# Audio tower on one core: masked k blocks by DMA, conv and down as rounded products, weights rounded between the first slots

## What is computed

```python
# tokens: a conv of kernel 2 and stride 2, the mean of the pair added, layer norm
x = einsum('btki,oik->bto', xb, conv_w) + conv_b + xb.mean(axis=2)
h = layernorm(x) * gamma + beta
# attention over the batch of 64, 16 heads of 16
q, k, v = split(layernorm(h) @ qkv.T + qkv_bias)
h = h + softmax(q @ k.T / 4) @ v @ out_proj.T + out_bias
# gated feed-forward, weights and activations rounded to FP4 in blocks of 16
def fp4(x):                      # per block of 16
    scale = maximum(max(abs(x)) / 6, 1e-12)
    return GRID[searchsorted(MID, abs(x / scale))] * sign(x) * scale
z = layernorm(h)
g = silu(fp4(z) @ fp4(w_gate).T) * (fp4(z) @ fp4(w_up).T)
h = h + fp4(g) @ fp4(w_down).T
```

## Time and profile before

| | |
|---|---|
| Median of 3 runs | 4660.76 us (4659.73 to 4663.47) |
| The profiled execution | 4667.47 us, of it a span of 4665.6 us |
| PE busy | 4432.7 us, 95% of the span |
| DVE busy | 3333.5 us, 71% |
| ACT busy | 2640.0 us, 57% |
| POOL busy | 1959.1 us, 42% |

### The profile page before, as it was taken

How to read it: one execution, slowest core, us unless ns; L and a number is a source line. 1 busy time by engine, 2 the same in 40 slices (tenths; PEclk the granted TensorE clock), 3 DMA queues, 4 the chain that set the end, 5 groups by cost and what they waited for, 6 DMA issues and landing times.

```text
span 4665.6 us, 119233 instructions
## 1 busy us (share of the span) xinstructions
PE 4432.7 (95%) x43016; PEld 3952.5 (85%) x43016; DVE 3333.5 (71%) x6915; ACT 2640.0 (57%) x5596; POOL 1959.1 (42%) x2582
## 2 busy tenths in 40 slices
PE   3999999999999985999999999999999999999997
PEld 2888888888888864899999999999999999998986
DVE  4888888888888863566666666666666666666665
ACT  2666666666666643455555555555555555555553
POOL 1455555555555531334334334334334334334333
PEclk9999999999999997999999999999999999999998
DMA  2000000000000001000000000000000000000000
GB/s 84 20 24 20 24 24 24 22 22 24 24 24 21 23 15 39 8 8 8 15 9 8 15 9 8 15 9 8 15 9 8 15 9 8 15 9 8 15 5 11
DMA packets 64945, 79.30 MB, mean 17 GB/s; under 512 B 8758, under 2 KB 51126, under 8 KB 64438
## 3 DMA queue, kind: packets, MB, share of 16 engines
q1 hardware_dynamic: 64566, 74.07, 5.4%
HBM read 49.40 MB, written 24.64 MB: 16 GB/s over the span
## 4 chain that ended last, share of the span: by engine, by line
PE 56%; DVE 2%; issue 1%; ACT 1%; POOL 1%; DMA 0%; ACTq 0%; DVEq 0%; SPq 0%; POOLq 0%
PE bA L938 11%; PE bA L939 9%; PE bA L940 9%; PE bS L1223 4%; PE bO L1245 3%; PE bA L1307 3%; PE bB L938 2%; PE bB L1208 2%; PE bB L1209 2%; PE bB L940 2%; PE bB L939 2%; PE bA L1308 2%; PE bT L1261 2%; PE bO L1254 1%; PE bO L1249 1%
## 5 line engine op out<-in xcount | busy, mean ns | idle before, releaser
L1638 POOL TENSOR_TENSOR sqs_lo<-sq,sqs_hi 128x768 fp32r<-128x768 f32 x256 | 477.9, 1867 | 676.7 <-ACT sqs_hi L1358 673.1
L1449 DVE TENSOR_TENSOR qk_lo<-bA,qk_hi 128x384 fp32r<-128x384 f32 x512 | 284.5, 556 | 538.6 <-ACT qk_hi L1358 538.5
L1377 ACT ACTIVATE phi<-bB 128x768 f32<-128x768 f32 x256 | 207.4, 810 | 665.1 <-PE bB L1209 665.1
L1596 POOL TENSOR_TENSOR yT_lo<-tanh_y,yT_hi 128x384 fp32r<-128x384 f32 x256 | 259.4, 1014 | 556.8 <-ACT yT_hi L1358 556.8
L1358 ACT ACTIVATE qk_hi<-bA 128x384 fp32r<-128x384 f32 x512 | 251.6, 491 | 203.7 <-PE bA L940 203.5
L1459 DVE TENSOR_TENSOR aT<-bS,mask 128x1024 f32<-128x1024 f32 x256 | 311.0, 1215 | 2.0 <-PE bS L1228 1.3
L1367 ACT ACTIVATE sq<-bA 128x384 f32<-128x384 f32 x512 | 250.3, 489 | 62.0 <-DVE qk_lo L1449 61.8
L518 PE MATMUL bank<-down_sb,hqT 128*128 128x256 f32 x1128 | 278.7, 389 | 1.0 <-ACT hqT L600 1.0
L616 ACT ACTIVATE kblk<-gu,kb_masked,rowmask 128x128 f32<-128x128 f32 x752 | 271.3, 463 | 8.1 <-PE gu L542 8.1
L518 PEld LDWEIGHTS bank<-down_sb,hqT 128*128 128x128 f32 x1128 | 204.3, 190 | 52.8 <-issue 32.6
L938 PE MATMUL bA<-fc_lo,yT_hi 128*128 128x256 f32 x768 | 230.6, 300 | 12.9 <-ACT pre L1407 6.2
(11 more groups left out here) (245 smaller groups left out, 15104.2 us busy)
## 6 DMA issues: line engine op xcount, KB each, us to landing
xT<-in_x SPq DMA_DIRECT2D x94, 256.0 KB, 2.6
h_scratch<-h SPq DMA_DIRECT2D x188, 64.0 KB, 1.9
hx<-h_scratch SPq DMA_DIRECT2D x32, 256.0 KB, 2.7
out<-res SPq DMA_DIRECT2D x32, 256.0 KB, 2.2
hx<-h_scratch SPq DMA_DIRECT2D x64, 64.0 KB, 2.5
out<-res SPq DMA_DIRECT2D x64, 60.0 KB, 1.8
q<-in_fc_q SPq DMA_DIRECT2D x2, 1024.0 KB, 6.4
wq_sb<-in_wq SPq DMA_DIRECT2D x1, 1024.0 KB, 5.0
```

The lines of the kernel that those rows point to most:

```text
L1449: dve.tensor_tensor(dst, src, hi.bitcast(fp32), ALU.subtract).then_inc(S[done], 1)
L1638: pool.tensor_tensor(sqs[1][:], sq[:], sqs[0][:].bitcast(fp32), ALU.subtract).then_inc(S["sq_lo"], 1)
```

## The change

1. **k by DMA.** qk_product computes k first, into a bank of its own. ACT copies it once into `kT` (two instructions), right after probs_copy. SP then issues eight DMAs, each of 16 partitions, that put kT's pieces into a `kblk` cleared once at the start. scores waits for all eight, besides q.
2. **Conv and down rounded.** Both go over `product3`. x is split by a copy on ACT (`x_copy`) and a subtraction on POOL (`x_low`), a slot ahead; hq's transpose by ACT's copy and a new subtraction on DVE (`hq_low`), between glu_up and h1_add.
3. **Order.** DVE: the maximum of xq, then h2_add, then xq's scales. POOL: hq's scaling ahead of h0b.
4. **Weights between slots.** The prologue's block goes. `slots` calls `weights(t)` ahead of each of the first six slots, and the loads, the rounding (two steps now in place of four, the scalings on POOL, the magnitude on ACT), transposes and splits of the weights are spread over them. SP loads layer 1's 4 MB ahead of slot 5.

The core of the diff:

```diff
+                def k_blocks(t):                                    # SP
+                    wait_step(sp, "qk_copied", t, QK, KC)
+                    for j in range(4):
+                        for r in range(2):
+                            p = slice(64 * r + D0 * j, 64 * r + D0 * (j + 1))
+                            sp.dma_start(kblk[p, :, j, :], kT[p, :, :]).then_inc(S["kblk_ready"], 16)
                 def slot(t, par):
                     if exists(t, -1):
                         load(t + 1, 1 - par)
                     if exists(t, 4):
                         store(t - 4, par)
+                    if exists(t, 0):
+                        k_blocks(t)
+                def weights(t):
...
+                    if t == 5:
+                        for dst, v in (("wq_sb", wq), ("wk_sb", wk), ("wv_sb", wv), ("wo_sb", wo)):
+                            sp.dma_start(w1[dst][:], v.rearrange("(c p) n -> p c n", p=128)).then_inc(w1_loaded, 16)
                 def conv(t, par):                                   # PE
-                    pe.wait_ge(S[f"x_loaded{par}"], t * 8 + (16 - 8 * par))
+                    wait(pe, "x_low", t + 1)
                     for c in range(2 * KC):
-                        last = pe.matmul(cv[:, 0:DM], xT[par][:, c, :], conv_sb[:, c, :], start=c == 0,
-                                         stop=c == 2 * KC - 1)
+                        last = product3(pe, cv[:, 0:DM], [x[:, c, :] for x in xTs], [w[:, c, :] for w in conv_w0],
+                                        c == 0, c == 2 * KC - 1)
                 def scores(t):
                     wait(pe, "qk_copied", t, QK)
+                    wait(pe, "kblk_ready", t, 16 * KB)
                     wait(pe, "att_step", t - 1, ATT)
                 def down(t):
-                    wait(pe, "hqT_copied", t - 3, 2)
+                    wait(pe, "hqT_split", t - 3, 2)
                     for f, (o, w) in enumerate(F0C):
-                        last = pe.matmul(cv[:, 0:DM], hqT[0:w, f, :], down_sb[0:w, f, :], start=f == 0,
-                                         stop=f == len(F0C) - 1)
+                        last = product3(pe, cv[:, 0:DM], [x[0:w, f, :] for x in hqT], [x[0:w, f, :] for x in down_w0],
+                                        f == 0, f == len(F0C) - 1)
                 def qk_product(t):
-                    for w, o in ((q_sb, 0), (k_sb, 256)):
+                    for b, w in ((1, k_sb), (0, q_sb)):
...
-                    last.then_inc(S["qk_done"], 1)
+                        last.then_inc(S["qk_done"], 1)
                 def k_copy(t):                                      # ACT
-                    wait(act, "qk_done", t + 1)
+                    wait_step(act, "qk_done", t, 2, 1)
                     wait(act, "scores_done", t)
                     for c in range(KC):
-                        src = gu[:, 0, 256 + 128 * c:256 + 128 * (c + 1)].rearrange("p (n k) -> p n k", n=2)
-                        for j in range(4):
-                            act.activation(kblk[:, c, :, j, :], src, ACT.Identity, bias=kb_masked[:, c, j:j + 1],
-                                           scale=rowmask[:, j:j + 1]).then_inc(S["qk_copied"], 1)
+                        act.activation(kT[:, c, :], gu[:, 1, 128 * c:128 * (c + 1)], ACT.Identity,
+                                       bias=kb_col[:, c:c + 1]).then_inc(S["qk_copied"], 1)
+                def x_copy(t, par):
+                    act.wait_ge(S[f"x_loaded{par}"], t * 8 + (16 - 8 * par))
+                    wait(act, "conv_done", t)
+                    copy(xTs[0][:], xT[par][:], "x_high")
                 def slot(t, par):                                   # ACT
                     if exists(t, 1):
                         v_copy(t, 1 - par)
+                    if exists(t, -1):
+                        x_copy(t + 1, 1 - par)
...
                         probs_copy(t)
+                    if exists(t, 0):
+                        k_copy(t)
                     if exists(t, 2):
                         xq_magnitude(t)
+                def hq_low(t):                                      # DVE
+                    wait(dve, "hqT_copied", t - 3, 2)
+                    dve.tensor_tensor(hqT[1][:, 0:5, :],
+                                      pt[:].rearrange("p a b -> p (a b)")[:, 0:640].rearrange("p (f t) -> p f t", t=128),
+                                      hqT[0][:, 0:5, :].bitcast(fp32), ALU.subtract).then_inc(S["hqT_split"], 1)
+                    dve.tensor_tensor(hqT[1][0:64, 5, :], pt[0:64, 1, 128:256], hqT[0][0:64, 5, :].bitcast(fp32),
+                                      ALU.subtract).then_inc(S["hqT_split"], 1)
                     if exists(t, 2):                                # DVE's slot
-                        x_st = xq_scales(t - 2)
-                        xq_scaled(x_st)
+                        x_st = xq_amax(t - 2)
                     if exists(t, 4):
                         h2_add(t - 4, par)
+                    if exists(t, 2):
+                        xq_scales(x_st)
+                        xq_scaled(x_st)
+                def x_low(t, par):                                  # POOL
+                    wait(pool, "x_high", t + 1)
+                    pool.tensor_tensor(xTs[1][:], xT[par][:], xTs[0][:].bitcast(fp32), ALU.subtract)\
+                        .then_inc(S["x_low"], 1)
+                def weights(t):                                     # POOL
...
+                    if t == 1:
+                        weight_scaled("gate")
+                        weight_scaled("up")
+                        pool.wait_ge(wfold, 5 + KC)
+                    if t == 2:
+                        weight_values("gate")
+                        weight_values("up")
+                        weight_scaled("down")
+                    if t == 3:
+                        weight_values("down")
```

More of the change, by code:

```diff
@@ L107, in fp4_scales @@
     st.add(dve.reciprocal(inv, inv))
+def fp4_scales(dve, st, x, small, rows, width, gain=1.0):
+    fp4_amax(dve, st, x, small, rows, width)
+    fp4_inverse(dve, st, small, rows, width, gain)
 def fp4_scaled(eng, out, x, small, k, rows, width):
@@ new lines, in layer0 @@
+        wconv, wsmall, wqkv, wout = sem("wconv"), sem("wsmall"), sem("wqkv"), sem("wout")
+        wconst, vones, wfold, vbias = sem("wconst"), sem("vones"), sem("wfold"), sem("vbias")
+        wconv_hi, wconv_lo = sem("wconv_hi"), sem("wconv_lo")
+        wpad, wtrans, whigh, wlow = sem("wpad"), sem("wtrans"), sem("whigh"), sem("wlow")
+        W = {n: {k: sem(f"{n}_{k}") for k in ("loaded", "scales", "scaled", "abs", "round", "ready")}
+             for n in ("gate", "up", "down")}
+        wraw = {"gate": sb("graw", [128, GROUPS, DM]), "up": sb("uraw", [128, GROUPS, DM]), "down": sb("draw", [128, KC, F0])}
@@ L388, in wait_stored, with slots @@
                 eng.wait_ge(S[f"{name}{par}"], t * 16 + (32 - 16 * par))
-        def slots(eng, slot):
+        def slots(eng, slot, weights):
             first = 6
@@ L394, in slots @@
             for t in range(first):
+                weights(t)
                 slot(t, t % 2)
@@ L590, in slot, with weight_rows @@
                         pv_product(t, 1 - par)
-                pe.wait_ge(wfold, 6 + 2 * KC)
-                pe.wait_ge(wcopied, len(JOBS))
-                pe.wait_ge(wlow, 2)
-                slots(pe, slot)
+                def weight_rows(n, c, bank):
+                    o = bank[:].rearrange("p a b -> p (a b)")
+                    for j in range(GROUPS):
+                        rows = 128 if j < GROUPS - 1 else LAST
+                        last = pe.transpose(o[:, 128 * j:128 * j + rows], wraw[n][0:rows, j, 128 * c:128 * (c + 1)],
+                                            ident[0:rows, 0:rows])
+                    last.then_inc(wtrans, 1)
@@ L597, in _ @@
+                slots(pe, slot, weights)
             @block.scalar
@@ L660, in ln1_copy @@
                     copy(ln1T[:], tp[:, 0:256], "ln1T_copied")
+                    if isinstance(t, int) and t == 0:
+                        weight_magnitude("gate")
                 def probs_copy(t):
@@ L894, in _ @@
+                slots(dve, slot, weights)
             @block.gpsimd
```

377 lines of the change are left out of this document (212 added, 165 removed).

## The result

The changed kernel takes 4966.57 us (median of 4 runs, 4961.49 to 4972.83) against 4661.43 (4 runs, 4659.73 to 4663.47) of the kernel before: ratio 1.0655, 95% interval 1.0637 to 1.0673. It is 305 us slower, and 249 us above the upper end of the forecast's range.

A forecast was written before the change was run, and what follows sets the result against it. TensorE was taken to bound the 17.18 us slot, then k's DMA chain at 17.25: +6 us over about 88 slots, -24 from the prologue, -18 in sum, a median of 4643 us, range 4590 to 4718.

The forecast's parts named there:

- What bounds the kernel: First layer's steady loop: TensorE sets today's 17.18 us slot by a small margin, with DVE waiting only four or five times.
- DVE's count: First layer's loop: if the DMA chain is cheap, DVE sets a 16.8 us slot, total 4604; chance 0.27.
- the one for TensorE: First layer's loop: TensorE's work alone gives a 15.9 us slot, total 4527; chance 0.02.
- Part 1: Conv and down as rounded products on TensorE: conv 1.92 to 1.42, down 2.87 to 2.12, 1.25 us less per slot.
- Part 2: DVE between glu_up and h1_add: hq_low adds 0.82 + 0.29 less overlap, 1.0 us, of which 0.41 fills h1_add's wait.
- Part 3: Reordering on POOL and DVE: hq's first rounding step falls from 1.30 to 0.9 us, 0.4 us gone.
- Part 4: k's blocks by DMA: first issue +12.57, issues 0.44 apart, landing 1.45, so T = 17.25, +6 us over about 88 slots.
- Rival C: TensorE in the loop: the wait drops its clock to 1.2 GHz, T about 19, 4800 or more; chance 0.05.
- A: k's DMA chain: dearer, 0.475 per issue and 1.8 to land, T = 17.85, total 4696; chance 0.33.
- The sum: Whole kernel: +6 from the loop and -24 from the prologue give -18, a median of 4643 us.
- Part 5: Weights between slots: first conv about 10 us, seventh near 150, 30 us for weights, 10 us ACT hole; gain taken 24.
- A with the stores in the way: k's DMA chain: dearer DMA prices with the stores also in the way, T = 18.1, total 4718.

The follow-up runs named there:

- k4_dmas: Changed kernel, but SP issues only four of k's eight DMAs, the other blocks staying zero: 4626.41 us, ratio 0.9926.
- k1_dma: Changed kernel, but only one of k's eight DMAs is issued, seven eighths of the blocks staying zero: 4625.67 us, ratio 0.9919.
- warm_wait: Changed kernel, all eight DMAs, plus ten unused fp32 128x128 matmuls on TensorE just ahead of scores' wait for k: 4832.17 us, ratio 1.0368.
- flat_blocks: Changed kernel with kblk laid out so each transfer writes one 1 KB piece per partition instead of two of 512 B: 4960.58 us, ratio 1.0650.
- k_by_act: Changed kernel with ACT's eight masked copies of k back in their old place instead of the DMAs: 4758.27 us, ratio 1.0217.
- two_queues: Changed kernel with four of k's eight DMAs issued by ACT behind its two copies, four by SP: 4952.97 us, ratio 1.0627.
- pool_mask: Changed kernel with k's blocks made by two POOL multiplications of kT with a 0/1 mask instead of the DMAs: 4711.42 us, ratio 1.0112.
- sp4_pool: Changed kernel with SP transferring two of four k blocks, POOL masking the others, layer 1's weight loads one to a slot: 4656.39 us, ratio 0.9988.
- nudged: sp4_pool plus two tiny unused POOL additions ahead of its 128x768 subtraction in each layer 1 slot's last chunk: 4641.49 us, ratio 0.9969.

## Why the prediction was wrong

- **What bounds the kernel, and DVE's count.** Near. Without the chain the slot is 16.67 to 16.69 (k4_dmas, k1_dma); the count for DVE had said 16.8 and the one for TensorE 15.9. That 16.8 fits is in part luck, since TensorE is as full there, and its own count was too low, by 0.47 from part 1 alone.
- **Part 1.** Right in direction, too large: down takes 708.36 - 705.97 = 2.39 (forecast 2.12; before 2.87), conv 714.37 - 712.75 = 1.62 (forecast 1.42; before 1.92), 0.78 us a slot and not 1.25. The price of 0.118 us holds inside a group, but single steps at its start or end, and where the rows change from 128 to 64, take some 0.2. In the changed kernel this is no gain in time, since the wait for k swallows it; where the chain is off the path the slot is 0.5 shorter than before (k4_dmas).

```profile
705.97 0.28 PE L1051 MATMUL bank<-down_lo,hqT_hi 128*128 128x256 f32 x1
...
708.36 0.44 PE L342 MATMUL bank<-ident,ln 128*128 128x128 f32 x2
...
712.75 0.39 PE L1051 MATMUL bank<-conv_lo,xT_hi 128*128 128x256 f32 x1
...
714.37 1.14 PE L351 MATMUL gu<-v_sb,ln1T 128*64 128x128 f32 x16
```

- **Part 2.** Right: 0.82 + 0.27, and h1_add with no wait.
- **Part 3.** Right: hq's first step takes 0.91 instead of 1.30.
- **Part 4, the step that failed, in three terms.** Place and structure were right: scores wait for eight issues in a row and the last landing. (a) The issue. I took 0.44 from one to the next, from 0.35 to 0.48; measured (5.18 - 0.59)/7 = 0.66. That is 1.5 us, and above the range. No row I had was of a transfer between two tensors in SBUF, but the price was in the trace of the kernel before. I took the duration of layer 1's stores (0.35) and a small gap; the time from one start to the next is some 0.57 even there (0.92 less 0.35). Nearer are the two stores of the same slot, 1.18 us together: they start 0.70 apart. (b) The landing. I took 1.45 and measured 1.9, the upper end: 0.45 us. It is what those two stores take as well. The rows of the kernel before, with the second store by itself:

```profile
707.52 0.48 SPq L414 DMA_DIRECT2D h_scratch<-h  x1
...
2057.51 0.92 SPq L1174 DMA_DIRECT2D out<-res  x2
...
h_scratch<-h SPq DMA_DIRECT2D x188, 64.0 KB, 1.9
```

By 0.70 and 1.9 the chain gives T = 12.57 + 4.90 + 1.9 + 0.15 = 19.52, and the sum 4843; warm_wait, the same chain at full clock, has 18.99 and 4832. The Trainium skill gives 2.0 us whatever the size ("DMA: Bandwidth & Descriptors", section "Anatomy of one DMA"), measured there on transfers that GpSimd issues. The trace shows 1.9 for SP's, and I had weighed size and target above it.

(c) The clock. Rival C had the mechanism and a chance of 0.05, since I judged it by a wait of 0.7 to 1 us, that is, by my own mid value of the chain. The wait is 2.4 us. At the dear end of my range (18.0) it would have been 1.4 to 1.7, and at 19.52 some 3: C was no rival of A, it grows with A. Measured price 1.49 us a slot (warm_wait). In the slot the first issue comes at +13.85, and in warm_wait at +12.40 (710.94 against scores at 717.53 - 18.99), where I had +12.57.

- **The sum again with measured terms:** 13.85 + 4.59 + 1.9 + 0.15 = 20.49; the mean slot is 20.48. With warm_wait's first issue it is 12.40 + 4.59 + 1.9 + 0.15 = 19.04; warm_wait has 18.99.
- **Part 5.** First conv at 8.77 (forecast 10), seventh at 157.84 (150), 17.4 us gained of the forecast 24 to 25. ACT's hole is 14.6 us and not 10: the load of x's tile is itself held 4.30 us at its issue behind the 4 MB, which I hadn't counted. With slots of 17.18 the rest leaves 157.8 - 8.8 - 103.1 - 14.6 = 31 us for the weights, forecast 30; but k's transfers lie on these slots too (k1_dma has its seventh conv at 151.2), so the two can't be told apart here.
- **Not forecast at all:** 13 us in layer 1. A pair of operations changed order there, but that the time is theirs is not shown.
- **The range.** Its dear end was A with the stores in the way; these never were (they are out at 711.53, and kT is ready at 711.54). A had 0.475 for an issue, which was not the highest row: the stores' 0.70 was. And nothing in the range stood for A and C together.

## What to carry to other kernels

Eight small transfers in a row are priced here per issue: 0.66 us from one to the next for 16 KB each between two SBUF tensors, and 1.9 us for the last to land. Read such a price from start to start, not from the duration of an issue, and from the transfers that stand on the same queue in the same loop: two stores of the kernel before had 0.70 and 1.9. Where rows of one kind disagree (0.48, 0.57, 0.70), the dearest needs a chance of its own. And if TensorE waits behind such a chain in every slot, ask next what its clock does: here the rival "the wait is longer" and the rival "the clock falls" were one case, and some idle matmuls ahead of the wait show in a run which part is which.

## What the runs showed of the hardware

- With 2.2 to 2.5 us idle in each slot of 20.5, TensorE's granted clock fell to 0.50 for 3.4 us in every slot, 1.49 us lost. It fell 0.3 us ahead of the end of the wait in the changed kernel and 1.4 us behind it in flat_blocks. With 1.4 us idle in a slot (k_by_act) it stayed 1.00. In two_queues two shorter waits, 0.9 and 1.3 us between 718.9 and 722.6, were followed by the same.
- An issue within SBUF of 16 partitions costs 0.59 us (0.66 from one to the next), whether with pieces of 512 B or 1 KB; a 64 KB store to memory costs 0.48 in the kernel before (0.70 from one to the next, with two register operations between). SP and ACT issue side by side at about that price, and ACT does nothing else meanwhile (two_queues). What sets the price was not tested beyond the pieces.
- An operation of DVE with two inputs in SBUF takes 0.70 to 1.15 us instead of 0.43 beside one of POOL (pool_mask, sp4_pool), and 2.08 instead of 0.55 when it starts 0.15 us behind. Two operations of 0.2 us ahead of POOL's turned that order round in layer 1 and took 15 us off the kernel (nudged against sp4_pool), 8 of them in the slots at the turn.
